# Output rows of a 32-cell attention kernel as seven block products of 256 columns in three groups

## What is computed

```python
o = transpose(_chunk_abc(q, k, v, s))                # b, t, 16 heads, 128
g = (hidden_states @ Wg).reshape(b, t, H, DV)
o = o * rsqrt(mean(square(o), axis=-1, keepdims=True) + EPS) * g_norm_weight
o = o * (g * sigmoid(g))
attn = o.reshape(b, t, VALUE_DIM) @ Wo               # 2048 x 512
x = layernorm(x + attn)
```

## Time and profile before

| | |
|---|---|
| median of three runs | 1337.4 us (1337.39 to 1337.41) |
| profiled execution, its own time | 1337.4 us |
| its span in the profile | 1335.7 us |
| TensorE matmul, weight load | 1326.4 us (99%), 1143.3 us (86%) |
| VectorE, ScalarE, GpSimd | 813.2 us (61%), 473.0 us (35%), 276.4 us (21%) |
| output rows: matmuls of 512 columns | 768, in 32 groups of 24 |
| additions of the rows on VectorE (L742) | 128 of 0.685 us |
| granted TensorE clock, mean | 0.999 of full speed |

### The profile page before, as it was taken

How to read it: one execution, slowest core, us unless ns; L and a number is a source line. 1 busy time by engine, 2 the same in 40 slices (tenths; PEclk the granted TensorE clock), 3 DMA queues, 4 the chain that set the end, 5 groups by cost and what they waited for, 6 DMA issues and landing times.

```text
span 1335.7 us, 20339 instructions
## 1 busy us (share of the span) xinstructions
PE 1326.4 (99%) x8160; PEld 1143.3 (86%) x8160; DVE 813.2 (61%) x1559; ACT 473.0 (35%) x1391; POOL 276.4 (21%) x254
## 2 busy tenths in 40 slices
PE   9999999999999999999999999999999999999998
PEld 7888888888888888888888888888888888888886
DVE  5665666556666565656655566666556667656754
ACT  5333333343333433333234333343333333432221
POOL 3012311132112301231113111231023113122211
PEclk9999999999999999999999999999999999999999
DMA  6000200010000100010001000010000210000010
GB/s 205 17 1 0 56 1 16 1 32 25 16 1 25 32 17 1 9 48 5 12 0 48 10 17 1 25 32 17 1 22 27 64 33 0 1 0 32 18 46 32
DMA packets 35357, 31.73 MB, mean 24 GB/s; under 512 B 7617, under 2 KB 28097, under 8 KB 35265
## 3 DMA queue, kind: packets, MB, share of 16 engines
q1 hardware_dynamic: 35264, 30.44, 7.6%
HBM read 26.24 MB, written 4.19 MB: 23 GB/s over the span
## 4 chain that ended last, share of the span: by engine, by line
PE 97%; DVE 1%; DMA 0%; ACT 0%; issue 0%; POOLq 0%; SPq 0%; POOL 0%
PE p L899 20%; PE p L901 19%; PE p L900 19%; PE t L948 5%; PE s L973 3%; PE o L1090 3%; PE xb L1045 2%; PE o L1026 2%; PE o L1024 2%; PE t L1090 2%; PE p L973 2%; PE s L1379 2%; PE s L1381 2%; PE s L1380 2%; PE xb L998 2%; PE o L1023 2%
## 5 line engine op out<-in xcount | busy, mean ns | idle before, releaser
L899 PE MATMUL p<-wvg_hi,xt_hi 128*128 128x512 f32 x512 | 206.0, 402 | 0.1
L900 PE MATMUL p<-wvg_lo,xt_hi 128*128 128x512 f32 x512 | 199.8, 390 | 0.0
L901 PE MATMUL p<-wvg_hi,xt_lo 128*128 128x512 f32 x512 | 199.8, 390 | 0.0
L542 ACT ACTIVATE v_tok<-p 128x256 f32<-128x256 f32 x128 | 49.8, 389 | 318.8 <-PE p L901 318.8
L708 DVE SCALAR_TENSOR_TENSOR gate<-th,p 128x256 f32<-128x256 f32 x128 | 54.0, 422 | 164.4 <-ACT th L546 160.9
L899 PE MATMUL p<-xt_hi,wsqk_hi 128*128 128x512 f32 x380 | 148.4, 391 | 0.0
L900 PE MATMUL p<-xt_lo,wsqk_hi 128*128 128x512 f32 x380 | 148.2, 390 | 0.0
L901 PE MATMUL p<-xt_hi,wsqk_lo 128*128 128x512 f32 x380 | 147.8, 389 | 0.0
L491 POOL TENSOR_TENSOR orstd<-ovar,minus_half 128x8 f32<-128x8 f32 x32 | 52.4, 1639 | 447.1 <-DVE ovar L843 447.1
L482 POOL TENSOR_TENSOR v_lo<-v_tok,v_hi 128x256 fp32r<-128x256 f32 x96 | 83.8, 886 | 198.9 <-ACT v_hi L551 198.9
L901 PEld LDWEIGHTS p<-wvg_hi,xt_lo 128*128 128x128 f32 x512 | 96.1, 188 | 21.3
(11 more groups left out here) (241 smaller groups left out, 2844.0 us busy)
## 6 DMA issues: line engine op xcount, KB each, us to landing
raw<-in_L_attn_Wv SPq DMA_DIRECT2D x32, 128.0 KB, 2.4
raw<-in_L_attn_Wg SPq DMA_DIRECT2D x32, 128.0 KB, 2.9
raw<-in_L_attn_Wo SPq DMA_DIRECT2D x16, 256.0 KB, 2.8
out<-acc SPq DMA_DIRECT2D x16, 256.0 KB, 2.1
acc<-in_L_attn_hidden_states SPq DMA_DIRECT2D x3, 1024.0 KB, 7.5
raw<-in_L_attn_Ws SPq DMA_DIRECT2D x8, 256.0 KB, 2.8
raw<-in_L_attn_Wq SPq DMA_DIRECT2D x8, 256.0 KB, 2.8
raw<-in_L_attn_Wk SPq DMA_DIRECT2D x8, 256.0 KB, 3.3
```

The lines of the kernel that those rows point to most:

```text
L542: nc.scalar.activation(v_tok[:, c, :], PB[bk][:, 0:VW], ACT.Copy).then_inc(v_done, 1)
L899: nc.tensor.matmul(out_, lh, rh, start=(k == 0), stop=False)
L900: nc.tensor.matmul(out_, lh, rl, start=False, stop=False)
L901: last = nc.tensor.matmul(out_, ll, rh, start=False, stop=(k == n - 1))
```

## The change

The rows of two chunks (256 tokens) and the two heads form a 2 x 2 block matrix A, the two heads and the two halves of 256 columns of Wo a 2 x 2 block matrix B. Instead of eight block products the change takes seven, by the scheme of Strassen and Winograd: with S1 = A21 + A22, S2 = S1 - A11, S3 = A11 - A21, S4 = A12 - S2 and the four sums T1 to T4 of B, the products are A11 B11, A12 B21, A22 T4, S1 T1, S2 T2, S3 T3, S4 B22. Each is three matmuls of 256 columns, for both chunk pairs 42 in all.

- TensorE: `output_rows` is replaced by three groups: `rows_first` (18 matmuls) in its place, `rows_second` (12) after `token_proj(2)` and `running_values(0)`, `rows_third` (12) after `token_proj(3)` and `running_values(1)`. Products of both chunk pairs share a bank: `U_BANK` (S2's partial sums are summed in PSUM over the three groups) and `C_BANK`. In cell 31 `token_proj(3)` and the turns of V come after `rows_third`. In the tail the groups follow each other directly.
- VectorE: four `add_rows` become seven additions (two `add_m24`, `add_m1`, `add_m5`, `add_u2`, `add_c`, and `add_u3` of double size); eight operations of 128 columns make the sums S (`y_sums`); `y_low` is 384 columns wide instead of 512; `y_low(0)` and `y_sums(0)` stand ahead of `keep_keys(2)`; `low_rows` is gone; in cell 30 `norm1_stats` stands ahead of `keep_values(1)`.
- ScalarE: a copy of one block, `a21`, ahead of each `yt_hi`; two copies of 512 columns for the high parts of S (`sums_high`); `rows_scaled` and four copies `rows_high` in the weight cells.
- GpSimd: two subtractions of 512 columns a cell (`sums_low`); in the weight cells four of 256 columns (`row_sums`) and four low parts of Wo (`row_lows`: 256, 512, 512, 512 columns).
- Memory: the new tiles share their place with ww_t, pz_t, rz_t and ws_t.

```diff
-P_USES = ["vg0", "vg1", "wo0", "wo1", "wo2", "wo3", "vg2", "vg3", "s", "q", "k", "a0", "a1"]
+P_USES = ["vg0", "vg1", "wo0", "wo1", "vg2", "vg3", "s", "q", "k", "a0", "a1"]
...
+        B11, B21, B22, T1, T2, T3, T4 = range(7)
+        A11, A12, A22, A21 = range(4)
+        S1, S2, S3, S4 = range(4)
...
+        U_BANK, C_BANK = SB[0], TB[0]
...
+        def row_sums(pool, J):
+            w1, w2 = row_pieces
+            t = sums[:].rearrange("p h a t -> p (h a t)").rearrange("p (k n) -> p k n", k=4)
+            pool.wait_ge(wo_scaled, 2 * (J + 1))
...
+            nc.gpsimd.tensor_tensor(t[:, 0, :], w1[:, HALF:D], w1[:, 0:HALF], ALU.subtract).then_inc(wo_summed, 1)
+            nc.gpsimd.tensor_tensor(t[:, 2, :], w2[:, HALF:D], w1[:, HALF:D], ALU.subtract).then_inc(wo_summed, 1)
...
+            nc.gpsimd.tensor_tensor(t[:, 1, :], w2[:, HALF:D], t[:, 0, :], ALU.subtract).then_inc(wo_summed, 1)
...
+            nc.gpsimd.tensor_tensor(t[:, 3, :], w2[:, 0:HALF], t[:, 1, :], ALU.subtract).then_inc(wo_summed, 1)
...
+        def sums_low(pool, prev, i):
+            pool.wait_ge(s_hi_done, prev.count(2, i + 1))
+            nc.gpsimd.tensor_tensor(s_lo[i][:], sums[:, i, :, :], s_hi[i][:].bitcast(F32),
+                                    ALU.subtract).then_inc(s_lo_done, 1)
...
+            if not first(cell):
+                sums_low(pool, cell.shifted(-1), 0)
 
             pool.wait_ge(e_tok_hi_done, cell.count(1, 1))
...
             for c in range(CH - 1):
+                if c == 1 and not first(cell):
+                    sums_low(pool, cell.shifted(-1), 1)
...
+            if wo_J is not None:
+                row_sums(pool, wo_J)
             if J is not None:
                 for i in range(3, 7):
                     split_low(pool, J, i)
+            if wo_J is not None:
+                row_lows(pool, wo_J)
...
-            nc.scalar.activation(yt_hi[:, half, :, :, :].rearrange("p c h t -> p (c h t)"), Y_BANK[half][:],
+            nc.scalar.activation(a21[:, half, :], Y_BANK[half][:, 3 * P:], ACT.Copy).then_inc(a21_done, 1)
+            nc.scalar.activation(yt_hi[:, half, :, :].rearrange("p a t -> p (a t)"), Y_BANK[half][:, 0:3 * P],
                                  ACT.Copy).then_inc(yt_hi_done, 1)
+
+        def sums_high(act, cell, half):
+            act.wait_ge(s_summed, cell.shifted(-1).count(8, 4 * half + 4))
+            nc.scalar.activation(s_hi[half][:], sums[:, half, :, :], ACT.Copy).then_inc(s_hi_done, 1)
...
+        def y_sums(dve, cell, half):
...
+            nc.vector.tensor_tensor(out_[:, S1, :], a21[:, half, :], blk[:, A22, :], ALU.add).then_inc(s_summed, 1)
+            nc.vector.tensor_tensor(out_[:, S3, :], blk[:, A11, :], a21[:, half, :], ALU.subtract).then_inc(s_summed, 1)
...
+            nc.vector.tensor_tensor(out_[:, S2, :], out_[:, S1, :], blk[:, A11, :], ALU.subtract).then_inc(s_summed, 1)
...
+            nc.vector.tensor_tensor(out_[:, S4, :], blk[:, A12, :], out_[:, S2, :], ALU.subtract).then_inc(s_summed, 1)
...
             keep_keys(1)
+            if not first(cell):
+                y_low(dve, cell, 0)
+                y_sums(dve, cell, 0)
             keep_keys(2)
             if not first(cell):
-                y_low(dve, cell, 0)
                 y_low(dve, cell, 1)
...
+            if not first(cell):
+                add_m24(dve, cell, 0)
             dve.wait_ge(ok_scaled, cell.count(1, 1))
             nc.vector.tensor_reduce(top[:], groups, AX_X, ALU.max).then_inc(top_done, 1)
             if not first(cell):
-                add_rows(dve, cell, 0)
+                y_sums(dve, cell, 1)
...
             if not first(cell):
-                add_rows(dve, cell, 1)
-            else:
-                keep_values(0)
+                add_m24(dve, cell, 1)
+                add_m1(dve, cell)
...
+            keep_values(0)
+            gate_vector(dve, cell, 2)
             if not first(cell):
...
+                add_m5(dve, cell)
+                add_u2(dve, cell)
+            if cell.b == CELLS - 2:
+
+                dve.wait_ge(added, CELLS - B + 1)
+                car.norm1_stats(dve, 0)
+            keep_values(1)
+            if not last:
+                gate_vector(dve, cell, 3)
+            if not first(cell):
+                add_c(dve, cell)
+                add_u3(dve, cell)
+            if last:
+                gate_vector(dve, cell, 3)
+                car.prep_low(dve, 0, PREP[0])
+                car.prep_low(dve, 1, PREP[1])
+            keep_values(2)
...
+            if last:
+                car.norm1_apply(dve, 0)
+                car.prep_low(dve, 2, PREP[2])
+                car.prep_low(dve, 3, PREP[3])
...
+        def row_product(out_, left, which, right, begin, done):
+            hi, lo = left
+            nc.tensor.matmul(out_, hi[:, which, :], wo_hi[:, right, :], start=begin, stop=True, skip_group_check=True)
+            nc.tensor.matmul(out_, hi[:, which, :], wo_lo[:, right, :], start=False, stop=True, skip_group_check=True)
+            mm = nc.tensor.matmul(out_, lo[:, which, :], wo_hi[:, right, :], start=False, stop=True, skip_group_check=True)
...
+        def rows_first(pe, cell):
...
+            for i in range(2):
...
+                pe.wait_ge(yt_lo_done, prev.count(2, i + 1))
+                row_product(PB[bk][:, 0:HALF], part, A12, B21, True, None)
+                row_product(PB[bk][:, HALF:D], part, A22, T4, True, m24_done)
+                row_product(U_BANK[:, i * HALF:(i + 1) * HALF], part, A11, B11, i == 0, m1_done if i == 1 else None)
+
+        def rows_second(pe, cell):
+            prev = cell.shifted(-1)
+            pe.wait_ge(s_lo_done, prev.count(2, 2))
+            for i in range(2):
+                row_product(C_BANK[:, i * HALF:(i + 1) * HALF], (s_hi[i], s_lo[i]), S1, T1, i == 0, m5_done if i == 1 else None)
+            pe.wait_ge(m1_read, prev.count(1, 1))
+            for i in range(2):
+                row_product(U_BANK[:, i * HALF:(i + 1) * HALF], (s_hi[i], s_lo[i]), S2, T2, False, u2_done if i == 1 else None)
+
+        def rows_third(pe, cell):
+            prev = cell.shifted(-1)
+            pe.wait_ge(m5_read, prev.count(1, 1))
+            for i in range(2):
+                row_product(C_BANK[:, i * HALF:(i + 1) * HALF], (s_hi[i], s_lo[i]), S4, B22, False, c_done if i == 1 else None)
+            pe.wait_ge(u2_read, prev.count(1, 1))
+            for i in range(2):
+                row_product(U_BANK[:, i * HALF:(i + 1) * HALF], (s_hi[i], s_lo[i]), S3, T3, False, a_done if i == 1 else None)
...
-                for c in range(CH):
-                    output_rows(pe, cell, c)
-            if last:
-                car.prep_turn(pe, 0, PREP[0])
-                car.prep_turn(pe, 1, PREP[1])
+                rows_first(pe, cell)
...
+            token_proj(pe, cell, 2)
             running_values(0)
-            token_proj(pe, cell, 2)
+            if not first(cell):
+                rows_second(pe, cell)
+            if not last:
+                token_proj(pe, cell, 3)
             running_values(1)
+            if not first(cell):
+                rows_third(pe, cell)
+            if last:
+                token_proj(pe, cell, 3)
+                pe.wait_ge(added, cell.count(1, 0))
+                car.prep_turn(pe, 0, PREP[0])
+                car.prep_turn(pe, 1, PREP[1])
             pe.wait_ge(pz_done, cell.count(1, 1))
             turned(PZ_BANK, [pz[:, c, :, :].rearrange("p h m -> p (h m)") for c in range(CH)], pz_turned)
+            running_values(2)
             if last:
                 for n in (2, 3):
                     pe.wait_ge(car.prep_lo, n - 1)
                     car.prep_turn(pe, n, PREP[n])
-            token_proj(pe, cell, 3)
-            running_values(2)
...
+            pe.wait_ge(c_read, CELLS)
...
+                    if g == 0 and t == 0:
+                        att.wait_tail_sums(pe)
```

More of the change, by code:

```diff
@@ L586, in cell_scalar @@
                 y_high(act, cell, 1)
-            if not first(cell):
+                sums_high(act, cell, 0)
                 act.wait_ge(ok_summed, cell.count(1, 1))
@@ L755, in cell_vector @@
+        def cell_vector(dve, cell, last=False):
             nxt = cell.shifted(1)
@@ L953, in turned_y @@
             pe.wait_ge(y_done, cell.count(2 * CH, 0))
[L954 to L966 removed]
+            a, b = 2 * half, 2 * half + 1
@@ L1132, in tail_turns, with tail_rows, wait_turn_banks, tail_sums_low @@
             turned_y(pe, Cell(None, CELLS), 1)
-        def tail_rows(pe):
+        def tail_rows(pe, h_done):
             pe.wait_ge(car.prep_lo, 6)
-            for c in range(CH):
-                output_rows(pe, Cell(None, CELLS), c)
+            pe.wait_ge(h_done, 2)
+            for rows in (rows_first, rows_second, rows_third):
+                rows(pe, Cell(None, CELLS))
+        def wait_turn_banks(pe):
+            pe.wait_ge(c_read, CELLS)
+        def tail_sums_low(pool):
+            sums_low(pool, Cell(None, CELLS - 1), 0)
```

(23 more changed lines are left out.)

238 lines of the change are left out of this document (145 added, 93 removed).

## The result

The changed kernel takes 1341.9 us (median of seven runs, 1341.3 to 1342.5) against 1337.4 (seven runs, 1337.3 to 1337.6): ratio 1.0033, 95% interval 1.0023 to 1.0043. Its profiled execution has a span of 1340.0 us, 4.3 more than before. (One further execution of the same kernel, measured later, took 1339.5; what differs there is told under "What makes the clock fall".) The difference is a sum of gains and losses of 1 to 10 us each, which follow.

The account below looks back on a forecast made before the run. TensorE's nearly gapless matmul stream, 97% of the chain, was taken as the bound. Common cells, weight cells, cell 30, cell 31 and tail: 1337.4 - 6.6 + 2.0 + 1.9 + 4.8 + 2.5 = 1342.0 us; forecast 1336 to 1347, range 1330 to 1350.

Parts of the forecast that it names:

- Matmuls removed: Output rows: 24 matmuls of 512 columns (5.49 us) become 42 of 256 (4.94), gross gain 0.55 us a cell.
- Third key sum: Common cell: VectorE's y_low(0) and y_sums(0) delay keep_keys(2), so TensorE waits 0.16 us; bounds 0.05 and 0.25.
- `s_lo`: Common cell: rows_second waits 0.17 us for the sums' low parts, a chain through three engines; bounds 0 and 0.45.
- Net of a common cell: Gross gain less two waits, 0.55 - 0.16 - 0.17 = 0.22 us; cells 1 to 30 give 6.6 us.
- Weight cells: Cells 0, 4, ... 28: GpSimd's fourth low part of Wo delays VectorE's scan; 0.25 a cell, 2.0 us, bounds 0 and 5.
- Cell 30: norm1_stats, 3.6 us on VectorE, ahead of keep_values(1) makes running_values(2) wait; cost 1.9 us, bounds 1 and 2.5.
- Cell 31: Without token_proj(3) as cover, VectorE's chain behind gate(3) delays the weights' scores; cost 4.8 us, bounds 3 and 6.
- Tail: Row groups follow each other directly and wait for low parts and additions; cost 2.5 us, bounds 1.5 and 4.
- The rival without waits in the common cell: Faster: both common-cell waits don't last, giving 1332.2 us; decides at 0.09 for both together; chance 0.20.
- The longer GpSimd chain: Slower: a GpSimd operation meets a two-input VectorE operation, 0.42 us more a common cell, giving 1354.6 us; chance 0.13.
- The weight loads: Slower: loads can't follow at 256 columns, recorded at 188 ns each, adding 92 us, 1434 in all; chance 0.02.

Follow-up runs that it names:

- the experiment gives the same 0.10: Changed kernel with the third keep_keys moved ahead of the fourth operation of y_sums(0): 1337.3 us (ten runs), ratio to the kernel before 1.0002.
- 619.07 to 624.21 in the experiment: Changed kernel with GpSimd's last low part of Wo in the weight cells waiting until VectorE's scan is done: 1341.0 us.
- the edit shows 1.0 of it: Changed kernel with the tail's fourth hidden product, hidden(0, 3), moved ahead of the three row groups: 1340.9 us.
- once an operation is moved: Changed kernel with the second pair's sums, y_sums(1), moved ahead of VectorE's row maximum: 1338.8 us (one run).

## Why the prediction was right, and where its steps were not

The forecast (slower, 1336 to 1347) was right, and the places where TensorE waits are the ones that it named. That the total agrees to 0.1 us (1342.0 against 1341.9) is luck. The common cells gained 3.0 more than predicted, the weight cells with cell 0 cost 1.0 less and the tail 0.2 less; against this, cell 30 cost 2.0 more, the stretch behind cell 31's wait 1.2, and the work after the tail 0.5. Most of the second group is the clock, which stood in no term, and which fell in cell 30 in one execution of this kernel and not in another: that one took 1339.5.

- **Matmuls removed.** Predicted 0.55 a cell, measured 0.47. The interval was taken from three in a row (0.117) and is 0.120 in a run, 0.13 a cell; the 24 before took 5.57 from their own start where I had multiplied 24 by 0.2287 (5.49), which gives 0.08 back.
- **Third key sum.** Predicted 0.16, measured 0.10. `hk` came 2.08 after the block copy where my sum of eight queue times had 2.12; the experiment gives the same 0.10.
- **`s_lo`.** Predicted 0.17, measured 0.055. The chain on the three engines was right (it ends 5.24 after the first row matmul, 5.20 by the sum); TensorE got there later than I had it, since 18 matmuls took 2.23 instead of 2.12. The slower interval that cost the gross gain hid this wait.
- **Net of a common cell.** Predicted 0.22, measured 0.32. This is the largest error in us: 3.0.
- **Weight cells.** The place and the mechanism hold from cell 4 on, the scan takes 2.07 (predicted 2.1), the cost is 0.11 a cell, not 0.25. The scan started on time; ww_t started 5.37 behind the scan's start (619.58 to 624.95), and 5.14 is when it is wanted (619.07 to 624.21 in the experiment), so it is 0.23 late, of which the predicted slack of 0.12 takes half. I had it 0.37 late because I added recorded lengths, and such instructions overlap a little. Cell 0 costs 0.20 where 0.25 was predicted, but not by this mechanism; the one wait there, for `hv`, is in no step of the prediction. (The Trainium skill, "SBUF — State Buffer", section "Who interferes with whom", has an instruction of VectorE with two inputs in SBUF and one of GpSimd that reads SBUF exclude each other. The rows agree for the scan, esq and `s_lo`, at 2.07, 0.69 and 1.73 against 1.23, 0.17 and 1.29.) `va` has a single input in SBUF and took longer beside GpSimd too, 1.23 against 0.28.
- **Cell 30.** The wait was priced at 1.9 and costs 2.24 (37.91 less 35.67). `va` beside GpSimd's low parts of the experts' weights took 0.95 more than the sum had for it; most of that was given back, because VectorE reached the statistics (1111.66) some 3.0 ahead of the time at which TensorE wanted the values (about 1114.7), and not 2.2. The 1.64 of the clock was in no term and is what puts the cell's 3.9 outside the bounds.
- **Cell 31.** Predicted 4.8, measured 4.9. The clock behind it was missed: 1.2 over before, 1.4 over the same stretch at full clock.
- **Tail.** Predicted 2.5, measured 2.3, by the waits in the order named (the edit shows 1.0 of it), but with `yt_lo(1)` the largest.
- **Missing.** The clock (1.64 and 1.4 us in the profiled execution, of which 2.8 shows against before), and 0.5 us in the 153 us from the turn of U to the end. The instructions there are the same. The 0.5 does not build up evenly: it comes in four steps of 0.15 to 0.22, all in the products of `ut` and `wt`, with 0.03 to 0.05 given back in between. In the first step, 20 intervals take 4.66 (1214.03 to 1218.69) where they took 4.54 (1210.18 to 1214.72); in the products of `x1t` that follow both kernels keep step. The same steps stand in the other profiles with the changed row products and not in that of the kernel before with its matmuls cut in two. Whether it is where the tiles lie in SBUF now, no run tests, and the cause stays open.

The rival without waits in the common cell falls: they last, 0.155 together, over the 0.09 from which it decided. The longer GpSimd chain did not come about, though its mechanism appears once an operation is moved. The weight loads follow at 0.120 in all runs of up to 48.

## What to carry to other kernels

Seven products for eight save what the matmuls' issue intervals say, and only if the sums' chains end before TensorE asks: here two waits ate a third of the gross gain (0.155 of 0.47 us a cell), and it came back by moving two blocks of VectorE's work, not by changing the arithmetic. Before moving a block of side work into a loop's last cells, ask what TensorE does meanwhile; a wait of 2 to 3 us there cost its length and, when the clock fell, 1.3 to 2.4 us more. And an experiment on a fall of the clock needs a repeat of the unedited kernel beside it.

## What the runs showed of the hardware

- The granted clock fell to its lower level behind idle times of 2.0 us (in four of eight executions), of 3.1 us (in eight of eight) and of 0.98 and then 1.41 us (in one of two), after hundreds of microseconds at full. In cell 30 the first matmuls after the wait were still fast (1116.85 to 1118.20). It cost 1.6 us in cell 30 and 1.3 to 2.4 in cell 31 (7.0 to 8.12 against 5.72).
- A matmul of 256 columns has an interval of 0.117 in a group of three and 0.120 in a run of 12 to 48, against 0.2287 for 512 columns: cutting 512 in two costs 5%.
- An instruction of VectorE on 8 or 4 columns a partition took 0.69 and 1.23 us instead of 0.17 and 0.28 beside a subtraction of GpSimd: the small size does not protect it.
